# Attention's first normalisers by logarithm, exponential and a Newton step, with new orders on three engines

## What is computed

```python
x = x + 0.5 * ffn(layernorm(x))          # top-1 of 8 experts: gate * (relu(x W1 + b1) W2 + b2)
x = x + attn(layernorm(x))
x = x + 0.5 * ffn(layernorm(x))

def attn(x):                             # inner layernorms have gain and bias
    h = layernorm(x, g1, b1)
    q, k, v = h @ wq, h @ wk, h @ wv     # 16 heads of 8
    phi_q, phi_k = elu(q) + 1, elu(k) + 1
    kv, z = sum_s(phi_k * v), sum_s(phi_k)
    x = x + ((phi_q @ kv) / (phi_q @ z + 1e-6)) @ wo
    h = layernorm(x, g2, b2)
    return x + table_gelu(round(h @ w1 / 0.1)) @ w2
```

## Time and profile before

| what | us |
|---|---|
| median of 3 runs | 220.37 (220.23 to 220.8) |
| profiled execution | 220.57 |
| its span, first to last instruction | 218.8 |
| busy in the span: PE, PEld | 191.8, 159.3 |
| busy in the span: DVE, ACT, POOL | 120.4, 111.6, 122.7 |

### The profile page before, as it was taken

How to read it: one execution, slowest core, us unless ns; L and a number is a source line. 1 busy time by engine, 2 the same in 40 slices (tenths; PEclk the granted TensorE clock), 3 DMA queues, 4 the chain that set the end, 5 groups by cost and what they waited for, 6 DMA issues and landing times.

```text
span 218.8 us, 4545 instructions
## 1 busy us (share of the span) xinstructions
PE 191.8 (88%) x1418; PEld 159.3 (73%) x1418; DVE 120.4 (55%) x506; ACT 111.6 (51%) x322; POOL 122.7 (56%) x190
## 2 busy tenths in 40 slices
PE   5998849999999985768977999999799899999991
PEld 2864339999999863656764588688444899999981
DVE  4687812222226527494865846757541566766652
ACT  2730006666555639849689875131300665666660
POOL 7861277765775788558311454558771154555544
PEclk9979988999999999999999999999969999999999
DMA  5999589899783120089991000001117919576700
GB/s 169 226 385 343 135 303 310 287 309 307 232 297 97 33 66 25 24 359 425 410 419 80 0 3 1 26 26 42 39 52 261 355 50 315 198 256 216 249 26 0
DMA packets 29753, 40.26 MB, mean 184 GB/s; under 512 B 4230, under 2 KB 20393, under 8 KB 28705
## 3 DMA queue, kind: packets, MB, share of 16 engines
q1 hardware_dynamic: 23968, 33.58, 43.2%
q0 software_dynamic: 2496, 4.76, 7.8%
q10 hardware_dynamic: 3264, 1.62, 2.6%
HBM read 10.78 MB, written 14.46 MB: 115 GB/s over the span
## 4 chain that ended last, share of the span: by engine, by line
PE 58%; POOL 12%; DVE 8%; SPq 6%; DMA 6%; issue 5%; ACT 4%; DVEq 0%; POOLq 0%; ACTq 0%
PE bank L937 15%; PE bank L949 14%; PE bank L1065 6%; PE bank L794 6%; PE bank L1081 5%; POOL xnT L566 3%; POOL rstd L507 3%; SPq L316 3%; PE bank L841 2%; PE bank L930 2%; SPq L376 2%; DMA rb<-in_L_ffn_router_b_dram 2%; DMA Xg<-xn_scratch,srcu 2%; DMA eqrq<-row_scratch 1%; DMA xnT<-slot_scratch,posu 1%
## 5 line engine op out<-in xcount | busy, mean ns | idle before, releaser
L650 ACT ACTIVATE hT<-bank,ewc_own 128x128 f32<-128x128 f32 x184 | 52.5, 368 | 62.4 <-PE bank L937 61.6
L937 PE MATMUL bank<-xT,ewc_own 128*128 128x128 f32 x368 | 50.2, 281 | 0.1
L949 PE MATMUL bank<-ew,hT 128*128 x368 | 48.8, 276 | 0.9 <-ACT hT L650 0.9
L937 PEld LDWEIGHTS bank<-xT,ewc_own 128*128 128x128 f32 x368 | 46.1, 197 | 0.7 <-issue 0.6
L949 PEld LDWEIGHTS bank<-ew,hT 128*128 128x128 f32 x368 | 44.8, 192 | 1.2 <-issue 1.2
L589 POOL DMA_INDIRECT out_dram<-ysb,eqrq x23 | 22.5, 979 | 29.7 <-DVE ysb L1319 27.1
L794 PE MATMUL bank<-ones_bf 128*128 128x512 bf16 x87 | 26.5, 440 | 3.7 <-POOL ident L452 2.6
L545 POOL DMA_INDIRECT Xg<-xn_scratch,srcu x23 | 22.0, 956 | 13.5 <-PE bank L930 5.4
L1298 DVE TENSOR_TENSOR ysb<-bank,ewc_own 128x128 f32<-128x128 f32 x23 | 6.7, 291 | 28.3 <-PE bank L949 24.1
L581 POOL DMA_INDIRECT row_scratch<-pay,posu x16 | 15.8, 988 | 10.9 <-DVE posu L1260 7.6
L566 POOL DMA_INDIRECT xnT<-slot_scratch,posu x16 | 15.7, 983 | 4.3 <-issue 4.3
(11 more groups left out here) (220 smaller groups left out, 304.8 us busy)
## 6 DMA issues: line engine op xcount, KB each, us to landing
ewc_own<-ew SPq DMA_DIRECT2D x46, 322.0 KB
row_scratch<-xn SPq DMA_DIRECT2D x8, 1024.0 KB, 10.5
ew<-in_L_ffn_W_dram SPq DMA_DIRECT2D x1, 2048.0 KB, 12.4
ew<-in_L_ffn_W_dram SPq DMA_DIRECT2D x8, 256.0 KB, 7.3
slot_scratch<-ysb SPq DMA_DIRECT2D x23, 64.0 KB, 2.0
eqrq<-row_scratch SPq DMA_DIRECT2D x15, 70.0 KB, 2.5
x<-in_L_attn_x_dram SPq DMA_DIRECT2D x4, 256.0 KB, 3.8
xn_scratch<-xn ACTq DMA_DIRECT2D x4, 256.0 KB, 6.3
```

Of the source, the lines that this page charges most:

```text
L650: last = A(hT[:, t.slot, c * P:(c + 1) * P], bank[2 + t.parity][:, c * P:(c + 1) * P], ACT.Relu, bias=ewc[t.ahead][:, B1_AT + c:B1_AT + c ...
L937: last = mm(bank[2 + t.parity][:, c * P:(c + 1) * P], ewc[t.ahead][:, c * P:(c + 1) * P], xT[:, t.slot, :], start=True, stop=True)
L949: last = mm(bank[4 + t.parity][:, 0:D], hT[:, t.slot, c * P:(c + 1) * P], ew[:, bass.ds(e[k], 1), W2_AT + c * D:W2_AT + (c + 1) * D].squee ...
```

## The change

The normalisers of kind "a" leave GpSimd. VectorE makes both variances plus epsilon (`first_variances`), ScalarE makes exp(-0.5 ln v) (`guess_rstd`), and VectorE improves that by one Newton step and makes the shift (`finish_rstd`). ScalarE loads a table set by name at its start. GpSimd only gathers. The orders of the attention rounds are new on ScalarE, VectorE and TensorE; the half of h1 of batch 0 that VectorE made goes to ScalarE. In both expert parts the last slot's `up` goes to two banks and signals each half. In the second, the factor 0.5 moves into the clipping, with b1 and b2 halved in advance, and the bias, gate and row are combined before y is there (`rest_of_rows`). Four of six `keep_warm` matmuls ahead of the rounds go. The keys of batch 0 now wait for the last y.

```diff
+        def up_bank(k, c):
+
+            return bank[6] if k + 1 == NT and c >= FC // 2 else bank[2 + k % 2]
...
-                    sp.wait_ge(y_ready, NT + 1 + k - UNROLL)
+                    sp.wait_ge(o_ready, 1 + k - UNROLL)
...
-            bring_back(0)
-            bring_back(1)
-            normaliser(LN_AT["a", 0] - 1)
-            bring_back(2)
-            normaliser(LN_AT["a", 1] - 1)
-            bring_back(3, range(GT // 2))
-            normaliser(LN_AT["a", 2] - 1)
-            bring_back(3, range(GT // 2, GT))
-            normaliser(LN_AT["a", 3] - 1)
+            for b in range(B):
+                bring_back(b)
             pool.wait_ge(w_in, 16 * 10)
             g.tensor_scalar(gb[:, 2:4], gb[:, 2:4], 10.0, None, ALU.mult).then_inc(gb_ready, 1)
-            g.tensor_scalar(ew[:, :, B2_AT:W2_AT], ew[:, :, B2_AT:W2_AT], 0.5, None, ALU.mult).then_inc(b2_halved, 1)
+            g.tensor_scalar(ew[:, :, B1_AT:W2_AT], ew[:, :, B1_AT:W2_AT], 0.5, None, ALU.mult).then_inc(b2_halved, 1)
...
-                    act.wait_ge(h_ps, m * NT + 1 + t.k)
+                    if k + 1 < NT:
+                        act.wait_ge(h_ps, m * (NT - 1) + 1 + t.k)
                     for c in range(FC):
-                        last = A(hT[:, t.slot, c * P:(c + 1) * P], bank[2 + t.parity][:, c * P:(c + 1) * P],
-                                 ACT.Relu, bias=ewc[t.ahead][:, B1_AT + c:B1_AT + c + 1])
+                        if k + 1 == NT and c % 2 == 0:
+                            act.wait_ge(last_ps, m * FC // 2 + 1 + c // 2)
+                        last = A(hT[:, t.slot, c * P:(c + 1) * P], up_bank(k, c)[:, c * P:(c + 1) * P],
+                                 ACT.Relu, scale=0.5 if m else 1.0, bias=ewc[t.ahead][:, B1_AT + c:B1_AT + c + 1])
                     last.then_inc(hT_ready, 1)
                     if m == 1:
                         chances(k)
+                    elif k == 20:
+                        guess_rstd(0)
+
+            def guess_rstd(b):
+
+                ts = slice(b * GT, (b + 1) * GT)
+                act.wait_ge(a_var, 2 * (b + 1))
+                A(alog[:, ts, :], avar[:, ts, :], ACT.Ln).then_inc(a_log, 1)
+                act.wait_ge(a_log, b + 1)
+                A(aguess[:, ts, :], alog[:, ts, :], ACT.Exp, scale=-0.5).then_inc(a_guess, 1)
...
+            nc.scalar.preload_act_table_set("natural_log_exp_and_others")
...
-                act.wait_ge(rstd_ready, LN_AT["a", b])
-                for t in range(b * GT, (b + 1) * GT if b else GT // 2):
+                act.wait_ge(a_ready, b + 1)
+                for t in range(b * GT, (b + 1) * GT):
...
+            normal1(0)
+            guess_rstd(1)
+            norm1(0)
+            normal1(1)
+            take_kv(0)
+            take_q(0)
+            norm1(1)
+            attention_input(0)
+            take_kv(1)
+            take_att(0)
+            guess_rstd(2)
+            take_q(1)
+            normal1(2)
+            attention_input(1)
+            norm1(2)
+            take_kv(2)
+            take_att(1)
+            take_q(2)
+            guess_rstd(3)
+            normal1(3)
+            attention_input(2)
+            norm1(3)
+            take_kv(3)
+            take_att(2)
+            take_q(3)
+            attention_input(3)
+            normal2(0)
+            norm2(0)
+            normal2(1)
+            normal2(2)
+            take_att(3)
...
-                        last = mm(bank[2 + t.parity][:, c * P:(c + 1) * P], ewc[t.ahead][:, c * P:(c + 1) * P],
+                        last = mm(up_bank(k, c)[:, c * P:(c + 1) * P], ewc[t.ahead][:, c * P:(c + 1) * P],
                                   xT[:, t.slot, :], start=True, stop=True)
-                    last.then_inc(h_ps, 1)
+                        if k + 1 == NT and c % 2 == 1:
+                            last.then_inc(last_ps, 1)
+                    if k + 1 < NT:
+                        last.then_inc(h_ps, 1)
...
-                        pe.wait_ge(y_ready, m * NT + t.k - 1)
+                        pe.wait_ge(o_ready if m else y_ready, t.k - 1)
...
-            keep_warm(6)
+            keep_warm(2)
...
+                if b == 0:
+                    pe.wait_ge(y_ready, NT)
...
+                if b == 0:
+                    turn1(1)
                 sum_kv(b)
-                if more:
+                numerators(b)
+                if b >= 1 and more:
                     turn1(b + 1)
-                numerators(b)
...
-                        v.scalar_tensor_tensor(out=ysb[:, t.k, :], in0=bank[4 + t.parity][:, 0:D], scalar=0.5,
-                                               in1=ewc[t.ahead][:, B2_AT:W2_AT], op0=ALU.mult, op1=ALU.add
-                                               ).then_inc(y_ready, 1)
+                        dve.wait_ge(dve_chain, rest_done[k])
+                        v.scalar_tensor_tensor(out=ysb[:, k, :], in0=bank[4 + t.parity][:, 0:D],
+                                               scalar=gate1[:, k:k + 1], in1=ysb[:, k, :], op0=ALU.mult, op1=ALU.add
+                                               ).then_inc(o_ready, 1)
...
-                def combine_rows(k):
+                rest_done = {}
+
+                def rest_of_rows(k):
+
                     t = Tile(k)
                     dve.wait_ge(ex1_ready, k + 1)
                     link(v.tensor_reduce(sum1[:, k:k + 1], ex1[:, t.ahead, :], AX, ALU.add))
                     link(v.reciprocal(gate1[:, k:k + 1], sum1[:, k:k + 1]))
-                    dve.wait_ge(y_ready, NT + 1 + k)
-                    v.scalar_tensor_tensor(out=ysb[:, k, :], in0=ysb[:, k, :], scalar=gate1[:, k:k + 1],
-                                           in1=Xp[:, t.ahead, 0:D], op0=ALU.mult, op1=ALU.add).then_inc(o_ready, 1)
+                    rest_done[k] = later(v.scalar_tensor_tensor(
+                        out=ysb[:, k, :], in0=ewc[t.ahead][:, B2_AT:W2_AT], scalar=gate1[:, k:k + 1],
+                        in1=Xp[:, t.ahead, 0:D], op0=ALU.mult, op1=ALU.add))
...
+                    if m == 1:
+                        rest_of_rows(k)
                     take_y(k)
-                    if m == 1:
-                        combine_rows(k)
-                    elif k in BACK:
+                    if m == 0 and k == 20:
+                        finish_rstd(0)
+                    if m == 0 and k in BACK:
                         take_back(BACK[k])
...
+            def first_variances(b):
+
+                ts = slice(b * GT, (b + 1) * GT)
+                for j in range(GT):
+                    last = v.bn_aggr(mv[:, b * GT + j, :], stat[:, j, :])
+                link(last)
+                v.tensor_scalar(avar[:, ts, 0:1], mv[:, ts, 1:2], 1.0, EPS, ALU.mult, ALU.add).then_inc(a_var, 1)
+                v.tensor_scalar(avar[:, ts, 1:2], mv[:, ts, 1:2], 1.0 + EPS, EPS * EPS, ALU.mult, ALU.add).then_inc(a_var, 1)
+
+            def first_statistics(b):
+
+                for j in range(GT):
+                    last = v.bn_stats(stat[:, j, :], x[:, b * GT + j, :])
+                link(last)
+                first_variances(b)
+
+            def finish_rstd(b):
+
+                ts = slice(b * GT, (b + 1) * GT)
+                dve.wait_ge(a_guess, b + 1)
+                link(v.scalar_tensor_tensor(out=astep[:, :, :], in0=aguess[:, ts, :], scalar=-0.5, in1=aguess[:, ts, :],
+                                            op0=ALU.mult, op1=ALU.mult))
+                link(v.tensor_tensor(out=astep[:, :, :], in0=astep[:, :, :], in1=avar[:, ts, :], op=ALU.mult))
+                link(v.scalar_tensor_tensor(out=rstd[:, ts, :], in0=astep[:, :, :], scalar=1.5, in1=aguess[:, ts, :],
+                                            op0=ALU.add, op1=ALU.mult))
+                v.scalar_tensor_tensor(out=shift[:, ts, :], in0=rstd[:, ts, :], scalar=-1.0,
+                                       in1=bc(mv[:, ts, 0:1], [P, GT, 2]), op0=ALU.mult, op1=ALU.mult).then_inc(a_ready, 1)
...
+            finish_rstd(1)
             phi_k(0)
-            begin(2)
             phi_q(0)
-            for b in range(B):
-                mask_kv(b)
-                if b >= 1:
-                    begin2(b - 1)
-                divide(b)
-                if b + 1 < B:
-                    phi_k(b + 1)
-                if b == 0:
-                    begin(3)
-                if b + 1 == B:
-                    quantise(0, range(3))
-                residual(b)
-                if b + 1 < B:
-                    phi_q(b + 1)
-            begin2(B - 1)
+            mask_kv(0)
+            combine(2)
+            divide(0)
+            first_statistics(2)
+            phi_k(1)
+            finish_rstd(2)
+            residual(0)
+            phi_q(1)
+            mask_kv(1)
+            combine(3)
+            divide(1)
+            first_statistics(3)
+            phi_k(2)
+            residual(1)
+            phi_q(2)
+            finish_rstd(3)
+            mask_kv(2)
+            begin2(0)
+            divide(2)
```

(33 more changed lines are left out.)

57 lines of the change are left out of this document (13 added, 44 removed).

## The result

| what | before | after |
|---|---|---|
| median of 20 runs each, in turn on one chip | 220.96 (219.52 to 222.66) | 219.61 (217.71 to 220.92) |
| profiled execution | 220.57 | 218.94 |
| its span | 218.8 | 217.2 |

The ratio is 0.9927, with a 95% interval of [0.9905, 0.9950]. On the 220.37 us that the forecast started from this is 1.6 us less (1.1 to 2.1 by the interval), 218.8, where 2.65 less, 217.7, was forecast; the two medians differ by 1.35. Faster by more than 0.3% was right; the size was not. Two more comparisons of the same two kernels, on other chips, gave 0.9892 [0.9844, 0.9940] and 0.9928 [0.9897, 0.9960].

A forecast was written before the change was run, and what follows sets the result against it. A chain of waits through several engines, not one full engine, was taken to bound the attention rounds. Savings of 1.65 and 1.0 us, 2.65 together, from 220.57, less 0.2 to the median, gave 217.7 us; range 216.5 to 219.7.

The forecast's parts named there:

- The end of the first experts: Before the rounds: up-projection at 72.0 us, last down-projection at 75.6 to 75.7, last y at 78.40 against 77.54.
- The small instructions: New normaliser instructions on VectorE cost 0.20 us each, ScalarE's logarithm and exponential 0.5 us a pair.
- Rival (a): Small instructions in the rounds cost more, 0.25 to 0.30 us on VectorE: 218.8 to 219.9 us; chance 0.12.
- Rival (b): ScalarE reloads tables for each logarithm and exponential pair: 220.8 us with one load, 225.4 with two; chance 0.05.
- The lead and its loss: Attention rounds: new order leads by 4.9, 3.9, then 1.6 us at numerators 1, 2, 3; normaliser 3 waits on VectorE.
- Rival (d): In the rounds the lead of 3.9 us is kept: up to 2.3 us more, 215.4 to 216.7 us; chance 0.10.
- GpSimd's queue: Gathers of batch 3 end near 87.4 us instead of 92.87, hidden by 4.7 us of cover before combine 3.
- The tail: End of the second experts: y's matmul-free half is computed earlier, so the last scatter starts at 215.13, 1.0 us sooner.
- the sum: Whole kernel: 1.65 us from the rounds plus 1.0 from the end of the second experts, 2.65 us less.
- rival (c): TensorE's clock falls in the rounds; one fall costs 1.4 us, giving 219.1 us; chance 0.08.

The follow-up runs named there:

- six fillers: Changed kernel with six instead of two keep_warm matmuls ahead of the attention rounds: 220.13 us, 0.9916 of the kernel before.
- the run of it alone: Kernel before with only the two expert-part edits (split last up-projection; bias, gate and row combined early, factor 0.5 in clipping): 219.49 us, 0.9953.
- once more: Changed kernel run again without an edit: 219.52 us, 0.9892 of the kernel before.
- third: Changed kernel run again without an edit, on another chip: 219.32 us, 0.9928 of the kernel before.
- filled rounds: Changed kernel with 3, 3 and 5 keep_warm matmuls ahead of keys 0, 2 and 3: 0.9987 on a disturbed chip, later 219.61 us, 0.9885.
- early normaliser 3: Changed kernel with finish_rstd(3) ahead of residual(1) on VectorE, guess_rstd(3) ahead of take_q(2) on ScalarE: 216.65 us (0.9837) and 216.53 us (0.9809).

## Why the prediction was right in direction and short in size

*The end of the first experts* was right. The up-projection (72.82) waits for the copy as forecast, and from it the whole last part can be counted: it lies 0.76 us later than the forecast's 71.76 plus 0.3, by the start of the run. With that taken off, the keys of batch 0 came at 79.3 (forecast 79.4), and the numerators at 84.6, 92.0, 101.4 and 111.2 (84.7, 92.2, 101.5, 111.1). The hole of the earlier trace rows at 76.01 is gone: the two down-projections are one row of 16.

*The small instructions* were right: 0.16 to 0.18 us long and 0.20 apart, 0.21 for logarithm and for exponential, and 0.44 from the start of the pair to its end, where 0.5 was taken. Rival (a) is out in the three profiles of the changed kernel as it stands; its bound of 0.25 to 0.30 us with GpSimd beside had no row, and the profile with six fillers has 1.00 and 0.93 for two such instructions. Rival (b) is out: ScalarE has the same three loads as before, the first at the start, the one of the earlier trace rows a little earlier, and one at 154.38, in the sorting (155.29 before, so the earlier trace rows is not the only one behind the start). ScalarE, after:

```profile
78.88 0.21 ACT L660 ACTIVATE alog<-avar 128x8 f32<-128x8 f32 x1 [0.89 <-DVE avar L1395]
79.11 0.21 ACT L662 ACTIVATE aguess<-alog 128x8 f32<-128x8 f32 x1
79.23 0.76 ACT L693 ACTIVATE h1T<-bank,gb 128x512 f32<-128x512 f32 x1
...
119.49 1.28 ACT L741 ACT_TABLE_LOAD   x1
```

*The lead and its loss* were right. It was forecast as 4.9, 3.9, 1.6; with the late start taken off it is 5.1, 4.0, 1.5. For the step from keys 3 to numerators 3 the forecast took its own track's 6.0 us over the 6.2 of the trace, and it measured 6.29; that is the missing 0.1. That normaliser 3 waits behind residual 1 and phi_q 2 was the reason given for most of the gain being lost again, and moving it brought 1.7 us. Rival (d) named the place where more was to be had, with up to 2.3 us; the order on VectorE kept the change from it, as argued.

*GpSimd's queue* was right: the gathers of batch 3 were issued from 80.84 to 84.62, and nobody waited for them. *The tail* was right: 0.9 in the profile and 1.0 us in the run of it alone.

*The step that failed* is that the sum put TensorE's clock at nothing, in two places. It carried the lead of 1.65 us unchanged from numerators 3 to the end, "since old and new order are the same from there", so the sorting was a term of zero. And it left a fall in the rounds to rival (c), which had one at 1.4 us with a chance of 0.08 because the old rounds had larger gaps "without a fall". The size of (c) was right (1.5 us, and numerators 3 at 112.75), the inference from one profile was not. The clock does not do the same in every execution: the old rounds have such a fall too, and it was free there only because GpSimd's chain was late anyway. Five profiles have the changed order in the rounds with nothing put into it (after, once more, third, with six fillers ahead, with ten less in the sorting); three of them have the fall at keys 3, all but the first and the third. That is 0.9 us on the average of the five, and 0.5 over the three of the kernel as it stands.

The second part of the loss is in the sorting. In the profiles after, once more, third, with six fillers and with filled rounds, PEclk over the seven microseconds of the fillers is 0.51 to 0.57 and ranks to first up takes 10.3 to 10.5 us. In the profiles of the kernel before (two), of its changed tail and of the early normaliser 3 (two, sound chips) it is near 0.76, and the stretch takes 9.4 to 9.6. That is 0.8 us, and rows 161.29 and 167.60 show its way to the path. Not all of it reaches the end. After a long sorting the second experts took 41.74 or 41.75 us from first to last up-projection, after a short one 41.75 to 42.67, with waits for rows as in the rows at 181.72 and 183.54. From the last ranks to the last up-projection the three profiles of the changed kernel average 52.13 us and the two of the kernel before 51.66: 0.5 us later. So of the 1.0 us that is missing in the ratio the falls in the rounds make 0.5 to 0.9 and the sorting about 0.5, as an estimate from these few profiles; which is the larger is not shown.

What stays open is why the clock falls as it does. The code of the sorting is the same in all of them. The low clock there is not tied to the order alone, since the early normaliser 3 had it once, on the disturbed chip. Nor do the clocks of all runs settle it: means of 0.962, 0.965 and 0.962 for the changed kernel in its three comparisons, against 0.969, 0.962 and 0.966 for the kernel before on three sound chips. So both losses are shown for the profiled executions; as the cause of the whole difference over 20 runs they are likely and not shown.

## What to carry to other kernels

Moving a short chain of small instructions from an engine that needs 1.69 us for its power alone to two engines with about 0.2 us for each instruction pays by its latency (1.3 us in the rounds here, without a fall). Then the in-order queue it lands in decides: put it in front of long work that only a later step needs, which was worth more than the move (1.7 us). Slack behind a slow engine also hides a slow clock, and who removes it pays for each fall; such a loss belongs into the sum with more than one profile of the kernel before behind it. Time won ahead of a stretch that is fed by loads can end there in a wait, so count to the end of that stretch and not to its start. Name the table set when two functions take turns on ScalarE.

## What the runs showed that was not expected

The clock fell, and for how long, differed between executions of one kernel: in the rounds at 105.6 us or not at all, in the first experts from 30 to 34 us or from 25 to 36. In the sorting it stayed low in the profile after through the first 4 us of matmuls back to back (the row at 161.29), while in the profile before it was back 2 us into them. And a higher mean clock was not always a shorter time: on top of the early normaliser fillers raised it by 0.006, and the ratio stayed as it was.
